# Cross-attention in a three-part layer: low parts of two short context units computed on GpSimd, and one softmax issued one key unit later

## The reference

```
q, k_new, v_new = LN(x) @ wq.T, LN(x) @ wk.T, LN(x) @ wv.T      # per batch 64 x 1024
k = concat(context, k_new); v = concat(context, v_new)          # per batch 1601 + 64 rows
attn = softmax(q @ k.T / 32)                                    # 64 x 1665
x = x + (attn @ v) @ wo.T
```

## Time and profile before

| what | value |
|---|---|
| three runs | 1269.29, 1269.14 and 1261.7 us, median 1269.14 |
| the profiled execution's own time | 1264.38 us |
| its span in the trace | 1262.6 us |
| attention in the trace | about 108 to 425 us |
| mean granted TensorE clock over the span | 0.987 of full speed |

### The profile page before, as it was taken

One profiled execution on the slowest core, in us unless ns is written; L12 is line 12 of the kernel. 1 busy time (PEld: TensorE's weight loads), 2 busy tenths in 40 slices (PEclk: granted clock), 3 DMA queues, 4 the chain that ended last, 5 costly groups with the idle time before them and its releaser, 6 DMA issues.

```text
span 1262.6 us, 19328 instructions
## 1 busy us (share of the span) xinstructions
PE 1200.4 (95%) x7810; PEld 1050.4 (83%) x7810; DVE 818.9 (65%) x1026; ACT 633.1 (50%) x604; POOL 95.7 (8%) x74
## 2 busy tenths in 40 slices
PE   5999999999998999999997699999999999999996
PEld 5888777777777878888886698989898999999895
DVE  7336789989999566463565674747565655656465
ACT  4124889888897423123543345344444444454431
POOL 0010000000000000000000012121111111121202
PEclk9999899999999999999999799999999999999998
DMA  7445899999998624220234376766667666676642
GB/s 290 146 159 192 308 352 360 376 373 363 379 383 333 248 77 171 96 100 34 101 143 167 113 251 166 262 197 226 202 216 212 200 227 200 217 210 230 172 160 33
DMA packets 46872, 272.98 MB, mean 216 GB/s; under 512 B 5880, under 2 KB 6024, under 8 KB 18528
## 3 DMA queue, kind: packets, MB, share of 16 engines
q1 hardware_dynamic: 36768, 243.48, 52.8%
q0 software_dynamic: 10048, 28.71, 9.4%
HBM read 255.92 MB, written 16.25 MB: 216 GB/s over the span
## 4 chain that ended last, share of the span: by engine, by line
PE 77%; DVE 8%; ACT 6%; issue 4%; DMA 4%; POOLq 0%; SPq 0%; POOL 0%; ACTq 0%; DVEq 0%
PE ps L1426 21%; PE ps L1427 21%; PE ps L1428 21%; PE ps L1539 6%; DVE lo L939 5%; ACT hi L628 4%; DMA out<-y,target 3%; PE ps L1652 2%; PE ps L1903 1%; PE ps L1587 1%; DVE stats L943 1%; ACT scores L692 1%; DMA raw<-weights 1%; PE ps L1745 1%; PE ps L1729 1%
## 5 line engine op out<-in xcount | busy, mean ns | idle before, releaser
L939 DVE TENSOR_TENSOR lo<-raw,hi 128x2048 fp32r<-128x2048 f32 (+1 forms) x198 | 443.4, 2251 | 160.3 <-ACT hi L628 157.9
L628 ACT ACTIVATE hi<-raw 128x2048 fp32r<-128x2048 f32 (+1 forms) x198 | 370.5, 1882 | 252.2 <-PE ps L1428 241.3
L1426 PE MATMUL ps<-act_hi,hi 128*128 128x240 f32 (+2 forms) x1232 | 360.7, 293 | 7.4 <-DVE act_lo L965 4.1
L1428 PE MATMUL ps<-act_hi,lo 128*128 128x240 f32 (+2 forms) x1232 | 361.6, 294 | 0.0
L1427 PE MATMUL ps<-act_hi,hi 128*128 128x240 f32 x1024 | 282.8, 276 | 0.0
L1426 PEld LDWEIGHTS ps<-act_hi,hi 128*128 128x128 f32 x1232 | 234.2, 190 | 16.7 <-issue 5.4
L1428 PEld LDWEIGHTS ps<-act_hi,lo 128*128 128x128 f32 x1232 | 234.6, 190 | 6.9
L1427 PEld LDWEIGHTS ps<-act_hi,hi 128*128 128x128 f32 x1024 | 193.5, 189 | 0.3
L1426 PE MATMUL ps<-hi,act_hi 128*128 128x512 f32 x320 | 126.4, 395 | 0.0
L1428 PE MATMUL ps<-hi,act_lo 128*128 128x512 f32 x320 | 124.9, 390 | 0.0
L1427 PE MATMUL ps<-lo,act_hi 128*128 128x512 f32 x320 | 124.8, 390 | 0.0
(11 more groups left out here) (228 smaller groups left out, 1431.2 us busy)
## 6 DMA issues: line engine op xcount, KB each, us to landing
raw<-weights SPq DMA_DIRECT2D x124, 1024.0 KB, 4.9
raw<-keys SPq DMA_DIRECT2D x36, 1024.0 KB, 5.8
raw<-context SPq DMA_DIRECT2D x31, 1024.0 KB, 8.3
raw_more<-context SPq DMA_DIRECT2D x17, 1024.0 KB
raw_more<-keys SPq DMA_DIRECT2D x12, 1024.0 KB
xq<-x_in SPq DMA_DIRECT2D x4, 512.0 KB, 6.8
raw_more<-weights SPq DMA_DIRECT2D x4, 512.0 KB
new_keys_t<-kvs POOLq DMA_DIRECT2D x8, 256.0 KB, 3.6
```

Source lines behind the costliest of these rows:

```text
L628: act.activation(part(hi, k, kind), part(raw, k, kind), ACT.Copy).then_inc(hi_done, 1)
L939: dve.tensor_tensor(part(lo, k, kind), part(raw, k, kind), part(hi, k, kind), ALU.subtract).then_inc(lo_done, 1)
L1426: pe.matmul(out, a_hi, b_hi, start=first, stop=False)
L1428: return pe.matmul(out, a_lo, b_hi, start=False, stop=last)
```

## The change

The subtractions of all `KEY_LAST` and `VALUE_LAST` units go from DVE to GpSimd, into one loop behind GpSimd's storing of the new keys. They count on a semaphore of their own, `tail_lo`; TensorE's `unit_ready` and SP's `load` wait for that semaphore where the unit is a short one, and for a correspondingly smaller count of `lo_done` elsewhere. `exps(0)` moves on ACT from behind the copy of unit 18 to behind the copy of unit 19. Helpers (`part`, `kind_of` and others) are moved up in the file without a change.

```diff
@@ load (SP)
-                    sp.wait_ge(lo_done, last + 1 + per * i)
+                    if kind_of(last) in (KEY_LAST, VALUE_LAST):
+                        sp.wait_ge(tail_lo, tails_before(last + 1))
+                    else:
+                        sp.wait_ge(lo_done, last + 1 - tails_before(last) + per * i)
@@ gpsimd, behind the stores of the new keys
+            for n in range(len(ATTENTION)):
+                k = U_KEYS0 + n
+                kind = kind_of(k)
+                if kind not in (KEY_LAST, VALUE_LAST):
+                    continue
+                pool.wait_ge(hi_done, k + 1)
+                if kind == KEY_LAST:
+                    (lo_a, lo_b), (raw_a, raw_b), (hi_a, hi_b) = (tail_parts(a, k) for a in (lo, raw, hi))
+                    pool.tensor_tensor(lo_a, raw_a, hi_a, ALU.subtract)
+                    pool.tensor_tensor(lo_b, raw_b, hi_b, ALU.subtract).then_inc(tail_lo, 1)
+                else:
+                    pool.tensor_tensor(part(lo, k, kind), part(raw, k, kind), part(hi, k, kind),
+                                       ALU.subtract).then_inc(tail_lo, 1)
...
+        def tails_before(k):
+            return sum(kind_of(m) in (KEY_LAST, VALUE_LAST) for m in range(U_KEYS0, min(k, U_WO)))
@@ attention (ACT), behind split(U_KEYS0 + n + AHEAD)
                     if what == "keys":
                         s = b - 1
+                        if u == 0 and s == 0:
+                            exps(0)
...
                             if b == 0:
                                 new_v_copy(copied)
                                 copied += 1
-                                exps(0)
@@ split (DVE)
+                if kind in (KEY_LAST, VALUE_LAST):
+                    return
                 dve.wait_ge(hi_done, k + 1 + per * i)
-                if kind == KEY_LAST:
-                    (lo_a, lo_b), (raw_a, raw_b), (hi_a, hi_b) = (tail_parts(a, k) for a in (lo, raw, hi))
-                    dve.tensor_tensor(lo_a, raw_a, hi_a, ALU.subtract)
-                    dve.tensor_tensor(lo_b, raw_b, hi_b, ALU.subtract).then_inc(lo_done, 1)
-                    return
@@ unit_ready (TensorE)
-                pe.wait_ge(lo_done, k + 1 + per * i)
+                if kind_of(k) in (KEY_LAST, VALUE_LAST):
+                    pe.wait_ge(tail_lo, tails_before(k + 1))
+                else:
+                    pe.wait_ge(lo_done, k + 1 - tails_before(k) + per * i)
```

More of the change, by code:

```diff
@@ L241, in perceiver_block @@
         lo_done = sem("lo_done")
+        tail_lo = sem("tail_lo")
         unit_used = sem("unit_used")
@@ L414, in landing, with part, half_tile, blocks_before @@
             return landed[slots[u]], 16 * (counts[u] + PER_EXPERT // RING)
+        def part(buf, k, kind):
+            whole = raw_of(k) if buf is raw else buf[:, k % RING, :]
+            if kind == KEY_LAST:
+                return whole[:, 0:C * (KTAIL + QL)]
+            if kind == VALUE_LAST:
+                return whole[0:KREM, 0:D]
+            if kind == BLOCK:
+                return whole[:, 0:D]
+            return whole
+        def half_tile(buf, h):
+            return buf[:, 4 * (h % 2):4 * (h % 2) + 4, (h // 2) * P:(h // 2 + 1) * P]
+        def blocks_before(n):
+            return sum(what == "block" for what, _, _ in ATTENTION[:n])
+        def tail_parts(buf, k):
+            whole = part(buf, k, KEY_LAST)
+            if buf is raw:
+                return (whole[:, 0:C * KTAIL].rearrange("p (c n) -> p c n", c=C),
+                        whole[:, C * KTAIL:].rearrange("p (c n) -> p c n", c=C))
+            by_chunk = whole.rearrange("p (c n) -> p c n", c=C)
+            return by_chunk[:, :, 0:KTAIL], by_chunk[:, :, KTAIL:]
+        def tails_before(k):
+            return sum(kind_of(m) in (KEY_LAST, VALUE_LAST) for m in range(U_KEYS0, min(k, U_WO)))
+        def kind_of(k):
+            if not U_KEYS0 <= k < U_WO:
+                return FULL
+            what, b, u = ATTENTION[k - U_KEYS0]
+            if what == "block":
+                return BLOCK
+            return FULL if u < 6 else (KEY_LAST if what == "keys" else VALUE_LAST)
         block = ctx.enter_context(nc.Block())
@@ L570, in rows_of_step @@
             return slice(QL * (s % 2), QL * (s % 2 + 1))
-        def part(buf, k, kind):
-            whole = raw_of(k) if buf is raw else buf[:, k % RING, :]
-            if kind == KEY_LAST:
[L576 to L604, removed]
         @block.scalar
```

## The result

| | before | after |
|---|---|---|
| median of 20 runs, us | 1264.03 (1259.99 to 1269.29) | 1270.13 (1267.41 to 1276.93) |
| profiled execution, us | 1264.38 | 1271.38 |
| its span, us | 1262.6 | 1269.6 |
| mean granted clock | 0.987 | 0.983 |

The ratio of after to before is 1.005, 95% interval 1.0035 to 1.0064: slower by 6.1 us between the medians. Forecast was a gain of 4.7 us as the likeliest case, 1262 as the time and 1255 to 1270 as the range. The sign was wrong, and the time lies just above the range.

What follows compares the result with a forecast made beforehand. Four resources were read as nearly level, so TensorE's waits decide; moved exponentials -3.4, batch 7 -1.3 and GpSimd 0 gave 1259.7 from 1264.38, 1264.4 on the median's scale; the middle, 1262, was taken, range 1255 to 1270.

Steps and rivals of the forecast that it cites:

- Moving `exps(0)`: ACT's exponentials behind the copy of unit 19: block ends at 145.9 instead of 149.33, gain 3.4 us if the clock stays up.
- I take it that it stays: TensorE's clock around units 19 and 20 was assumed to stay up after the move; if it falls, the gain is 1.4.
- The 2.0 us that the rival put on such a fall: Rival: the clock falls all the same at units 19 and 20, 1259.7 + 2.0 = 1261.7; chance 0.11.
- Gain 0 from the relief of DVE in steps 1 to 5 and in the short key units: Removing short subtractions from DVE only lengthens its idle time before ACT's copies there, so TensorE gains 0.
- The full relief (1249.5): Rival: relief of DVE counts everywhere, all `lo` waits but the 2.7 us already counted gone, 10.2 us; chance 0.05.
- Putting them on GpSimd ... Cost 0: Short subtractions on GpSimd, taken as T = 2.0 us, fit 4.2 us free at value units, 7 at key units: cost 0.
- the exclusion: Rival: GpSimd can't read two tiles while DVE does, at value unit 5; chance 0.20 DVE first, 0.14 GpSimd first.
- the sum as it stood: All terms over the whole kernel, -3.4 - 1.3 + 0 = 1259.7 on the profile's scale; chance 0.40.
- In all five batches: Steps 1 to 5: DVE's `lo` of value unit 5 about to begin (204.42) just as ACT's short copy ends (204.47).
- T - 1.65: Loss per batch at key unit 0, DVE first, T being GpSimd's subtraction time: 0.35 to 1.15 us; chance 0.20.
- T - 1.15: Loss per batch at value unit 5 and key unit 0, GpSimd first: 8.3 us over five at T = 2.8; chance 0.14.
- DVE being idle or reading PSUM at the others: Argument for the turns rival: pairs of two-tile reads by DVE and GpSimd exist only around value unit 5.

## Why the prediction was wrong, by its steps

**Moving `exps(0)`: right**, to 0.1 us (3.4); the new wait was 0.75 for 1.0. "I take it that it stays", of the clock, was right in this execution with some luck: of the eleven profiled executions with `exps(0)` moved, two (key units on GpSimd; all exponentials one copy later) show the clock at 0.76 and 0.80 over 136 to 143 us, and there the block ends 0.4 to 0.6 us later. The 2.0 us that the rival put on such a fall were too many.

**Gain 0 from the relief of DVE in steps 1 to 5 and in the short key units: right.** With the key units alone on GpSimd, or with writes in place of the value subtraction, the stretches of the table stay at 15.7 to 15.8 us. The full relief (1249.5) is refuted.

**"Putting them on GpSimd ... Cost 0": this step failed.** The duration was within its bounds (2.43; taken 2.0) and fits its cover of 4.2 us. But the sum took the two engines as independent. The only argument against the exclusion was that no row of before shows the two together, and that is no evidence either way; with it I gave the exclusion 0.34 and the sum as it stood 0.40. What the runs showed in its place: a two-tile subtraction on either engine waits for the one that runs on the other, and steps 1 to 5 lose 7.1 us. The traces agree with the rule that was set against them: the Trainium skill, "SBUF — State Buffer", SBUF: two separate sides, has one of the two wait for the other's whole instruction, and here each engine did so.

**"In all five batches" of the rival: it read step 1 and took it for all.** Before the change already, ACT's short copy ended 0.65 us after DVE's `qs` began in step 1 (204.47 against 203.82), but 0.28 us after it in step 2 (242.31 against 242.03). So in steps 1, 3 and 5 DVE had gone on to value unit 5 when GpSimd asked, and in 2 and 4 it was still in `qs`. The two branches came together; I had them as all or none. With DVE first the formula T - 1.65 gives 0.8 at T = 2.43; measured 0.47, since GpSimd held DVE only until 206.3. With GpSimd first T - 1.15 gives 1.3; measured 2.8 and 2.9. There the rival's term was mis-sized: TensorE waited 2.2 us more at value unit 5 (3.29 for 1.10), 0.6 of which replaced its old wait at key unit 0, and then lost 1.3 us to half clock (eight matmuls in 3.3 us instead of 1.97), which the formula left out. For the two steps 5.65 us came instead of 2.6. Without a fall of the clock the formula is nearly right: 1.5 us in step 5 of the run with GpSimd first.

**"DVE being idle or reading PSUM at the others": wrong.** The next unit's subtraction stands there (2.50 us, above), and so does the 64 x 64 scaling, held for 0.9 us in batch 7, which gave 0.3 us rather than 1.3. Moving it behind the scores gave that 0.9 us back (the wait fell from 1.30 to 0.42): from key unit 0 to value unit 0 of batch 7 it is 20.8 us there, 21.6 in the change and 21.9 before. So 1.2 of the 1.3 us were to be had.

**The scale and the range.** The median of before moved from 1269.14 in three runs to 1264.03 in twenty. On the latter the forecast of -4.7 would have been 1259.3; the time of 1262 was nearer only through the first three runs. The range was narrower than its own terms: rivals up to 1268 and a scatter of 4.9 above give 1273, and 1270 was written.

**What stays open** is 2 to 3 us. The medians differ by 6.1 us, the attention of the profiled executions by 4.0 without the later entry, and 1.2 of these 4.0 are the low clock at 412 us, which scatters. Falls of the clock that the one profile doesn't show, like that of the run with the value units alone, are a candidate: the runs' median clock is 0.9835, against 0.986 to 0.987 for the kernel before in the later sets. But the profiled execution has 0.983 itself, so this isn't shown.

## What to carry to other kernels

Work handed to an idle engine isn't free because that engine is idle; it can hold up the one it was taken from. Here 1.2 us of DVE work in slack became 2.4 us during which DVE and GpSimd couldn't both go on, and the large losses (2.8 and 2.9 us a step, against 0.5) stand where, of two requests 0.1 to 0.3 us apart, GpSimd's was first. Read every repetition of a pattern, not the first, where a race of that size decides. A wait should be priced with and without a fall of the clock behind it (2.8 and 1.5 us here). An offload placed where the other engine has slack, as the key units of steps 1 to 5, cost nothing, though the exclusion is there too.

## What the runs showed that I had not expected

- GpSimd's 65 x 1024 subtraction takes 2.43 us alone and 4.43 when DVE has just started a two-tile subtraction; DVE's 128 x 2048 one takes 2.29 and 4.49.
- A DVE scaling of 64 x 64 numbers from SBUF with a per-partition factor is held too: 1.16 us instead of 0.25.
- TensorE waits of 1.1, 0.4 and 1.05 us close together were followed by half clock for 3.4 us, twice in one execution, while a single wait of 1.59 us was not.
- The same waits aren't always followed by the same clock: a wait of 3.5 us at value unit 5 cost half clock in four steps of the run with GpSimd first and none in the fifth.
- A wait of 2.15 us in a stretch of narrow matmuls was followed, in the one execution that has it, by 13.7 us at half clock.
